# A rounding step by absolute value in bfloat16, and three of eight final tiles added by TensorE

## The chip, the core and the metric

The kernel runs on one NeuronCore of a Trainium2 chip. Five engines work side by side, each through its own queue in program order: TensorE (PE) multiplies matrices and writes to PSUM, VectorE (DVE) and ScalarE (ACT) work on tiles, GpSimd (POOL) here splits weights, and SyncE (SP) issues the transfers. They wait for one another by semaphores. The metric is the time of one execution on the device, in microseconds (us). Lower is better.

## The reference

`x` has 32 batches of 32 rows of 512. A per-batch 32x32 mix, chosen by a token, goes ahead of an attention block (32 heads, 8 key heads, rotary embedding, causal softmax, output projection), whose result is added to `x`. Then comes a second mix and one linear layer with values rounded to FP8, and that result is added as well:

```
x = x + attention(mix1(x))
y = mix2(x)
qinput, input_scale = per_tensor_quantize(y)       # scale = max|y| / 448
qinput = fp8_cast(qinput);  qw = fp8_cast(qweight)  # round to 3 mantissa bits
out = einsum(qinput * input_scale, qw * weight_scale) + bias
qout, out_scale = per_tensor_quantize(out)          # clip(out / scale, -448, 448)
x = x + qout * out_scale
```

Both quantizations need a maximum over the whole tensor, so each is a point that every tile has to reach before any can go on.

## The kernel before, in words

The 1024 rows are 8 tiles of 128 rows by 512 columns; `xacc` holds them in SBUF from the first load to the store. Up to about 496 us the attention runs, and TensorE is fed without a break. The order on each engine is written out by hand, function by function; waits are `wait_ge` on counting semaphores. The change touches the end of each engine's program.

Rounding to FP8 is done with additions. For a value v, ScalarE makes v and v times 2^20; from the latter `magic` keeps the exponent and sets one mantissa bit (an integer operation of VectorE), and two SCALAR_TENSOR_TENSOR of VectorE add and subtract the number, which leaves v rounded in bfloat16. `round_w8` (L1154) does it for four pieces of the weight matrix, between the last attention steps; ScalarE's part is `scale_w8` (L585). The loop at L1252 does it for the eight tiles of y: sum (L1257), difference (L1266), and, two tiles behind, the maximum of the layer's output (`f_largest`, L1240). `y_div` and `y_exp` are ScalarE's two outputs (L620, L624); tile 0's `y_exp` is made by VectorE (L1246).

TensorE's loop at L903: for tile 0 four products (L908) and the bias product (L910); for each later tile three products into the same bank whose values are overwritten and which keep the engine busy (`hold_clock`, L897), the bias product (L914), then four products (L917) once `y8_done` says that the tile is rounded. Then `spread_max(1)` (L891) transposes a column of maxima, so that each partition gets the maximum over all.

VectorE makes four columns from it, `col[:, 9:10]` the last of them. ScalarE's `f_divide` (L635) scales the eight tiles into `f_div`, VectorE clips each (`clip`, L1290), multiplies by the scale and adds `xacc` (`add_back`, L1295), and SP stores the tile (L348). The eight results lie in eight PSUM banks, `f_ps[0..7]` = banks 5, 0, 6, 7, 1, 2, 3, 4; before the spread writes to bank 5, ScalarE copies tile 0 to `f_keep`.

Of the kernel before, what the change touches and what calls it, by code (L numbers as in the profile page):

```python
# [78 lines left out]
def build(nc, x, itok, conds, wq, wk, wv, wo, qweight, w_scale, bias, consts, v_mem, out):  # L79
    with ExitStack() as ctx:  # L80
# [3 lines left out]
        def sem(name):  # L84
            return ctx.enter_context(nc.semaphore(name))
# [14 lines left out]
        with ExitStack() as products:  # L100
# [87 lines left out]
        scores_mm, s_turned, soft_step, exp_done = sem("scores_mm"), sem("s_turned"), sem("soft_step"), sem("exp_done")  # L188
        pv_mm, o_hi_done, o_lo_done, wo_mm, acc_done = (sem(n) for n in ("pv_mm", "o_hi_done", "o_lo_done", "wo_mm", "acc_done"))
        w8_scaled, w8_step, wT_mm, wT_done = sem("w8_scaled"), sem("w8_step"), sem("wT_mm"), sem("wT_done")  # L190
        y_mm, y_copied, y_amax, tail_mm, tail_vec = (sem(n) for n in ("y_mm", "y_copied", "y_amax", "tail_mm", "tail_vec"))
        y_div_done, y_exp_done, y8_magic, y8_sum, y8_done = (
            sem(n) for n in ("y_div_done", "y_exp_done", "y8_magic", "y8_sum", "y8_done"))
# [41 lines left out]
        y_exp = lambda t: wv_raw[1][:, t, :] if t < TPU else raw_o[:, t - TPU, :]  # L235
        f_div = y_exp
        f_keep = second_u[:]
        y_t = lambda t: y_kept[:, t, :] if t < TPU else y_ps[t][:]
        y_sum = [flat(p_tr), flat(s_nat[0])]
        tmp_scaled = [second_u[:], third_u[:]]  # L240
        tmp_sum = first_p[:]

        def left_part(h, i):

# [17 lines left out]
        def _(sp):  # L262
# [80 lines left out]
                sp.wait_ge(pv_mm, BPT * (2 * (KV - 2) + r + 1))  # L343
                load_values(KV - 1, r)

            for t in range(TILES):
                sp.wait_ge(result, t + 1)
                sp.dma_start(out_rows[t], xacc[:, t, :]).then_inc(dma_out, 16)  # L348
            sp.wait_ge(dma_out, 16 * TILES)

# [88 lines left out]
        def _(act):  # L439
# [145 lines left out]
            def scale_w8(c):  # L585
                act.wait_ge(dma_ffn, 16)
                if c >= 2:
                    act.wait_ge(w8_step, 3 * (c - 1))
# [39 lines left out]

            act.wait_ge(f_amax, 1)
            act.activation(f_keep, f_ps[0][:], ACT.Copy).then_inc(f_kept, 1)  # L630
            act.wait_ge(tail_vec, 9)

            def f_divide(t):

                act.activation(f_div(t), f_keep if t == 0 else f_ps[t][:], ACT.Copy,  # L635
                               scale=col[:, 9:10]).then_inc(f_div_done, 1)

            for t in range(TILES):
                f_divide(t)


        @block.tensor
        def _(pe):
# [199 lines left out]

            def turn_w8():

                pe.wait_ge(w8_step, 3 * KC)
# [38 lines left out]
            def spread_max(n):  # L885

                ps = w_ps[1] if n == 0 else f_ps[0]
                pe.wait_ge(tail_vec, 5 * n + 1)
                if n == 1:
                    pe.wait_ge(f_kept, 1)  # L890
# [12 lines left out]
            for t in range(TILES):  # L903
                if t == 0:
                    pe.wait_ge(wT_done, KC)
                    pe.wait_ge(y8_done, 1)
                    for c in range(KC):
                        pe.matmul(f_ps[t][:], y8[:, t, c * P:(c + 1) * P], wT[:, c, :], start=(c == 0), stop=False)  # L908
                    pe.wait_ge(bias_done, 2)
                    pe.matmul(f_ps[t][:], ones_r[:], bias_parts, start=False, stop=True).then_inc(f_mm, 1)  # L910
                else:

                    hold_clock(f_ps[t][:], 3)
                    pe.matmul(f_ps[t][:], ones_r[:], bias_parts, start=True, stop=False)  # L914
                    pe.wait_ge(y8_done, t + 1)
                    for c in range(KC):
                        mm = pe.matmul(f_ps[t][:], y8[:, t, c * P:(c + 1) * P], wT[:, c, :], start=False,  # L917
                                       stop=(c == KC - 1))
                    mm.then_inc(f_mm, 1)
            spread_max(1)  # L920


        @block.vector
        def _(dve):
# [229 lines left out]
            def round_w8(c):  # L1154

                dve.wait_ge(w8_scaled, c + 1)
                scaled, plain = tmp_scaled[c % 2], raw_w8[:, c, :]
                dve.tensor_scalar(scaled.bitcast(I32), scaled.bitcast(I32), EXP_BITS, HALF_BIT,
                                  ALU.bitwise_and, ALU.bitwise_or).then_inc(w8_step, 1)
                dve.wait_ge(w8_step, 3 * c + 1)  # L1160
                dve.scalar_tensor_tensor(out=tmp_sum, in0=scaled, scalar=LEAST, in1=plain, op0=ALU.max,
                                         op1=ALU.add).then_inc(w8_step, 1)
                dve.wait_ge(w8_step, 3 * c + 2)
# [64 lines left out]
            dve.wait_ge(tail_vec, 4)  # L1228
            dve.tensor_scalar(col[:, 2:3], col[:, 1:2], SHIFT, None, ALU.mult).then_inc(tail_vec, 1)

            def magic(t):

                if t > 0:
                    dve.wait_ge(y_exp_done, t)
                else:
                    dve.wait_ge(bias_step, 1)
# [12 lines left out]
            magic(0)  # L1249
            dve.wait_ge(bias_step, 2)  # L1250
            dve.reciprocal(col[0:BIAS_ROWS, 10:11], col[0:BIAS_ROWS, 8:9]).then_inc(bias_step, 1)
            for t in range(TILES):  # L1252


                dve.wait_ge(y_div_done, t + 1)
                dve.wait_ge(y8_magic, t + 1)
                dve.scalar_tensor_tensor(out=y_sum[t % 2], in0=y_exp(t), scalar=LEAST, in1=y_div(t), op0=ALU.max,  # L1257
                                         op1=ALU.add).then_inc(y8_sum, 1)
                if t == 0:
                    dve.wait_ge(bias_step, 3)  # L1260
                    dve.wait_ge(dma_ffn, 32)
                    dve.tensor_scalar(bias_sc, bias_row, col[0:BIAS_ROWS, 10:11], None, ALU.mult).then_inc(bias_done, 1)
                elif t < TILES - 1:
                    magic(t + 1)
                dve.wait_ge(y8_sum, t + 1)
                dve.scalar_tensor_tensor(out=y8[:, t, :], in0=y_exp(t), scalar=LEAST, in1=y_sum[t % 2], op0=ALU.max,  # L1266
                                         op1=ALU.subtract).then_inc(y8_done, 1)
                if t == 0:

                    dve.tensor_scalar(col[:, 5:6], col[:, 8:9], 1.0 / FP8_MAX, None, ALU.mult).then_inc(bias_step, 1)  # L1270
                    magic(1)
# [59 lines left out]
```

## Time and profile before

| | |
|---|---|
| time, median of 3 runs | 532.58 us (531.99 to 532.63) |
| the profiled execution | 532.47 us, span of its records 530.7 us |
| PE busy | 504.1 us (95%), 3150 products |
| DVE busy | 421.9 us (79%), 662 instructions |
| ACT busy | 247.9 us (47%), 475 instructions |
| POOL busy | 311.1 us (59%), 308 instructions |
| mean granted clock of TensorE | 0.988 |

The profile is of one execution. Its times count from the start of the span; 1.77 us of the execution lie outside it. A product of float32 leaves two records, others leave one. The record of a product contains its way through the array, so records overlap: what counts is the distance from start to start.

### The profile page before, as it was taken

How to read it: one execution, taken by the hardware profiler on the slowest of the kernel's cores; microseconds unless marked ns; L12 is line 12 of the kernel's file. 1: busy time of each engine (PE TensorE's matmuls, PEld its weight loads, DVE VectorE, ACT ScalarE, POOL GpSimd, SP SyncE). 2: the span in 40 equal slices, each digit the busy share in tenths (PEclk: the TensorE clock that was granted, in tenths of full speed). 3: DMA queues.
4: the chain of work that ended last, by engine and by line, in shares of the span. 5: the costliest groups of instructions: out<-in, count | busy, mean ns of one | idle time of the engine just before them, and what ended most of it. 6: DMA issues, size and time to landing. Idle time of an engine off the chain costs nothing.

```text
span 530.7 us, 9229 instructions
## 1 busy us (share of the span) xinstructions
PE 504.1 (95%) x3150; PEld 402.1 (76%) x3150; DVE 421.9 (79%) x662; ACT 247.9 (47%) x475; POOL 311.1 (59%) x308
## 2 busy tenths in 40 slices
PE   8988999998899999999999999999999999999990
PEld 6876877886688888888888888888888887788530
DVE  5469768796687969796979798978978788985796
ACT  2453454574163727472655346444635454333423
POOL 1238988689648765876597569756974653300000
PEclk9999999999899999999999999999999999999996
DMA  7315521220322031104020502040310005000004
GB/s 265 133 40 162 156 81 59 81 73 27 93 69 59 1 116 44 59 0 157 1 59 0 158 0 59 0 158 0 95 64 20 2 2 203 0 2 1 0 0 158
DMA packets 32644, 35.27 MB, mean 66 GB/s; under 512 B 2251, under 2 KB 22859, under 8 KB 32620
## 3 DMA queue, kind: packets, MB, share of 16 engines
q1 hardware_dynamic: 32620, 34.96, 20.5%
q8 instruction: 14, 0.23, 0.2%
q14 instruction: 10, 0.08, 0.0%
HBM read 28.66 MB, written 6.29 MB: 66 GB/s over the span
## 4 chain that ended last, share of the span: by engine, by line
PE 79%; POOL 11%; DVE 5%; issue 2%; ACT 1%; DMA 1%; DVEq 0%; ACTq 0%; POOLq 0%
PE bank L716 22%; PE bank L718 21%; PE bank L717 21%; POOL wq_lo L374 4%; PE bank L784 3%; PE bank L773 3%; POOL q_rot L388 2%; PE bank L840 1%; PE bank L659 1%; PE bank L917 1%; POOL o_lo L395 1%; POOL wo_lo L383 1%; PE bank L688 1%; DVE q_swap L1049 1%; PE bank L897 1%
## 5 line engine op out<-in xcount | busy, mean ns | idle before, releaser
L388 POOL TENSOR_TENSOR q_rot<-q_rot,q_swap 128x512 f32<-128x512 f32 x64 | 88.6, 1386 | 60.7 <-DVE q_swap L1049 60.7
L513 ACT ACTIVATE q_swap<-bank 64x512 f32<-64x512 f32 x80 | 47.6, 596 | 132.0 <-PE bank L718 84.5
L716 PE MATMUL bank<-wo_hi,o_hi 128*128 128x512 f32 x256 | 101.9, 398 | 4.4 <-issue 2.4
L718 PE MATMUL bank<-wo_hi,o_lo 128*128 128x512 f32 x256 | 100.5, 392 | 0.0
L717 PE MATMUL bank<-wo_lo,o_hi 128*128 128x512 f32 x256 | 100.3, 392 | 0.0
L1097 DVE TENSOR_TENSOR xacc<-xacc,bank 128x512 f32<-128x512 f32 x64 | 43.6, 682 | 37.5 <-PE bank L718 37.4
L1049 DVE TENSOR_TENSOR q_swap<-q_swap,cst 128x512 f32<-128x512 f32 x80 | 61.6, 769 | 0.0
L716 PEld LDWEIGHTS bank<-wo_hi,o_hi 128*128 128x128 f32 x256 | 48.3, 189 | 17.1 <-issue 4.8
L718 PEld LDWEIGHTS bank<-wo_hi,o_lo 128*128 128x128 f32 x256 | 48.3, 189 | 10.3
L717 PEld LDWEIGHTS bank<-wo_lo,o_hi 128*128 128x128 f32 x256 | 48.4, 189 | 9.6
L1048 DVE TENSOR_TENSOR q_rot<-bank,cst 128x512 f32<-128x512 f32 x64 | 43.8, 685 | 8.8 <-ACT q_swap L514 7.2
L383 POOL TENSOR_TENSOR wo_lo<-raw_o,wo_hi 128x512 fp32r<-128x512 f32 x32 | 45.0, 1429 | 9.7 <-ACT wo_hi L499 9.7
L716 PE MATMUL bank<-t_hi,wq_hi 128*128 128x512 f32 x128 | 49.8, 389 | 0.0
L718 PE MATMUL bank<-t_hi,wq_lo 128*128 128x512 f32 x128 | 49.8, 389 | 0.0
L717 PE MATMUL bank<-t_lo,wq_hi 128*128 128x512 f32 x128 | 49.8, 389 | 0.0
L374 POOL TENSOR_TENSOR wq_lo<-w_sum,wq_hi 128x256 fp32r<-128x256 f32 x64 | 48.4, 767 | 0.0
L514 ACT ACTIVATE q_swap<-bank 64x512 f32<-64x512 f32 x80 | 47.2, 591 | 0.9
L1090 DVE TENSOR_TENSOR o_lo<-bank,o_hi 128x512 fp32r<-128x512 f32 x64 | 39.6, 678 | 2.7 <-ACT o_hi L530 2.7
L374 POOL TENSOR_TENSOR wq_lo<-raw_q,wq_hi 128x256 fp32r<-128x256 f32 x48 | 36.7, 765 | 7.1 <-ACT wq_hi L482 7.1
L388 POOL TENSOR_TENSOR k_rot<-k_rot,q_swap 128x512 f32<-128x512 f32 x16 | 20.8, 1298 | 34.1 <-DVE q_swap L1049 34.1
L530 ACT ACTIVATE o_hi<-bank 128x512 fp32r<-128x512 f32 x64 | 33.1, 605 | 16.4 <-PE bank L784 16.1
L716 PE MATMUL bank<-hT_hi,wq_hi 128*128 128x512 f32 x96 | 39.1, 407 | 1.2 <-DVE v_st L963 1.0
(160 smaller groups left out, 1047.2 us busy)
## 6 DMA issues: line engine op xcount, KB each, us to landing
raw_q<-in_L_attn_wq SPq DMA_DIRECT2D x16, 512.0 KB, 3.9
raw_o<-in_L_attn_wo SPq DMA_DIRECT2D x8, 1024.0 KB, 7.4
v_st<-values SPq DMA_DIRECT2D x16, 256.0 KB, 4.4
xacc<-in_x SPq DMA_DIRECT2D x4, 512.0 KB, 7.0
raw_k<-in_L_attn_wk SPq DMA_DIRECT2D x8, 256.0 KB, 4.2
out<-xacc SPq DMA_DIRECT2D x8, 256.0 KB, 2.0
values<-v_more SPq DMA_DIRECT2D x6, 256.0 KB, 2.0
raw_o<-in_L_attn_wv SPq DMA_DIRECT2D x1, 1024.0 KB, 7.6
```

The source lines that it names most:

```text
L374: pool.tensor_tensor(wq_lo[:, i], left_part(h, i), wq_hi[:, i].bitcast(F32), ALU.subtract).then_inc(wq_lo_done, 1)
L383: pool.tensor_tensor(lo[:, h, :], raw_o[:, h, :], hi[:, h, :].bitcast(F32), ALU.subtract).then_inc(wo_lo_done, 1)
L388: pool.tensor_tensor(item_out(h, k), item_out(h, k), q_swap[(h + k) % 2][:], ALU.add).then_inc(rope_done, 1)
L513: act.activation(dst[0:P // 2, :], ps[P // 2:P, :], ACT.Copy)
L514: act.activation(dst[P // 2:P, :], ps[0:P // 2, :], ACT.Copy).then_inc(swap_done, 1)
L716: pe.matmul(dst, l_hi, r_hi, start=(i == 0), stop=False)
L717: pe.matmul(dst, l_hi, r_lo, start=False, stop=False)
L718: mm = pe.matmul(dst, l_lo, r_hi, start=False, stop=(i == n - 1))
L1048: dve.tensor_tensor(by_t(item_out(h, k)), by_t(item_ps[k][:]), cos_b, ALU.mult).then_inc(rope_cos, 1)
L1049: dve.tensor_tensor(by_t(q_swap[b][:]), by_t(q_swap[b][:]), sin_b, ALU.mult).then_inc(rope_mul, 1)
L1090: dve.tensor_tensor(by_batch(lo, b), by_tile(ps[b]), by_batch(hi, b).bitcast(F32), ALU.subtract).then_inc(o_lo_done, 1)
L1097: dve.tensor_tensor(xacc[:, tile, :], xacc[:, tile, :], w_ps[j % 2][:], ALU.add).then_inc(acc_done, 1)
```

## The change

In the rounding, ScalarE now writes `y_exp` and `tmp_scaled` as an absolute value in bfloat16 (Abs in place of Copy, a bfloat16 view on the same memory), and the integer operation is gone. Tile 0's `y_div` is made by VectorE and its `y_exp` by ScalarE, the other way round than before. `hold_clock` of a tile waits for `y_exp_done`.

In the last stretch the tiles 2, 4 and 6 (`BY_PE`) are added by TensorE: an identity product puts `xacc` into the banks of tiles 1, 2 and 3, whose values ScalarE has copied to SBUF before (`f_keep` for four tiles now); later a second product adds the clipped tile times an identity scaled by `col[:, 7:8]`, and ScalarE copies the bank to `xacc`. SP stores in the order `STORE_ORDER`.

```diff
-EXP_BITS = 0x7F800000
-HALF_BIT = 0x00400000
+BY_DVE, BY_PE = (0, 1, 3, 5, 7), (2, 4, 6)
+STORE_ORDER = (0, 1, 3, 2, 4, 5, 6, 7)
...
-        f_div = y_exp
-        f_keep = second_u[:]
+        f_div = lambda t: wv_raw[1][:, t, :] if t < TPU else raw_o[:, t - TPU, :]
+        y_exp = lambda t: f_div(t).bitcast(BF16)[:, 0:HID]
+        f_keep = lambda t: y_kept[:, t, :]
...
-        tmp_scaled = [second_u[:], third_u[:]]
+        tmp_scaled = [u[:].bitcast(BF16)[:, 0:HID] for u in (second_u, third_u)]
+        scaled_ident = first_p[:, 0:P]
...
-            for t in range(TILES):
-                sp.wait_ge(result, t + 1)
+            for t in STORE_ORDER:
+                if t in BY_PE:
+                    sp.wait_ge(act_result, BY_PE.index(t) + 1)
+                else:
+                    sp.wait_ge(result, BY_DVE.index(t) + 1)
...
-                act.activation(tmp_scaled[c % 2], raw_w8[:, c, :], ACT.Copy, scale=SHIFT).then_inc(w8_scaled, 1)
+                act.activation(tmp_scaled[c % 2], raw_w8[:, c, :], ACT.Abs, scale=SHIFT).then_inc(w8_scaled, 1)
...
                 if t == 0:
-                    act.wait_ge(tail_vec, 4)
-                act.activation(y_div(t), y_t(t), ACT.Copy, scale=col[:, 1:2]).then_inc(y_div_done, 1)
-                if t == 1:
                     act.wait_ge(tail_vec, 5)
-                if t > 0:
-                    act.activation(y_exp(t), y_t(t), ACT.Copy, scale=col[:, 2:3]).then_inc(y_exp_done, 1)
+                else:
+                    act.activation(y_div(t), y_t(t), ACT.Copy, scale=col[:, 1:2]).then_inc(y_div_done, 1)
+                act.activation(y_exp(t), y_t(t), ACT.Abs, scale=col[:, 2:3]).then_inc(y_exp_done, 1)
...
-            act.wait_ge(f_amax, 1)
-            act.activation(f_keep, f_ps[0][:], ACT.Copy).then_inc(f_kept, 1)
+            for t in range(TPU):
+                act.wait_ge(f_amax, t + 1)
+                act.activation(f_keep(t), f_ps[t][:], ACT.Copy).then_inc(f_kept, 1)
+
+            act.wait_ge(tail_vec, 8)
+            act.activation(scaled_ident, ident, ACT.Copy, scale=col[:, 7:8]).then_inc(spread, 1)
             act.wait_ge(tail_vec, 9)
...
+            for n, t in enumerate(BY_PE):
+                act.wait_ge(pe_sum, n + 1)
+                act.activation(xacc[:, t, :], f_ps[n + 1][:], ACT.Copy).then_inc(act_result, 1)
...
+                    pe.wait_ge(y_exp_done, t + 1)
                     hold_clock(f_ps[t][:], 3)
...
+            for n, t in enumerate(BY_PE):
+                pe.wait_ge(f_kept, n + 2)
+                pe.wait_ge(f_amax, n + 2)
+                pe.matmul(f_ps[n + 1][:], ident, xacc[:, t, :], start=True, stop=False)
             spread_max(1)
+            pe.wait_ge(spread, 1)
+            for n, t in enumerate(BY_PE):
+                pe.wait_ge(f_clip, t + 1)
+                pe.matmul(f_ps[n + 1][:], scaled_ident, f_div(t), start=False, stop=True).then_inc(pe_sum, 1)
...
-                dve.tensor_scalar(scaled.bitcast(I32), scaled.bitcast(I32), EXP_BITS, HALF_BIT,
-                                  ALU.bitwise_and, ALU.bitwise_or).then_inc(w8_step, 1)
...
-            def magic(t):
...
-                dve.tensor_scalar(y_exp(t).bitcast(I32), y_exp(t).bitcast(I32), EXP_BITS, HALF_BIT,
-                                  ALU.bitwise_and, ALU.bitwise_or).then_inc(y8_magic, 1)
...
-            dve.tensor_scalar(y_exp(0), y_t(0), col[:, 1:2], SHIFT, ALU.mult, ALU.mult).then_inc(bias_step, 1)
+            dve.tensor_scalar(y_div(0), y_t(0), col[:, 1:2], None, ALU.mult).then_inc(bias_step, 1)
...
-                magic(t + 1)
...
             clip(0)
-            for t in range(1, TILES):
-                clip(t)
-                add_back(t - 1)
-            add_back(TILES - 1)
+            clip(1)
+            add_back(0)
+            clip(2)
+            add_back(1)
+            clip(3)
+            add_back(3)
+            clip(4)
+            clip(5)
+            clip(6)
+            clip(7)
+            add_back(5)
+            add_back(7)
```

How the queues stand at the end of the program. First TensorE before, from tile 7's holding products on (`bank4` is tile 7's bank, `bank5` takes the spread; L897 is `hold_clock`, L914 the bias, L917 the tile's products, L891 the spread):

```order
L897 MATMUL bank4<-w8 128x512 x3
L914 MATMUL bank4<-wk_hi,ones_r 128x512
L917 MATMUL bank4<-wT,y8 128x512 [waits y8_done]
L917 MATMUL bank4<-wT,y8 128x512 x3
L891 MATMUL bank5<-cst,col 128x128 [waits f_kept,tail_vec]
```

And TensorE now, from the same place (L906, L924, L927 and L900 are the same four; `cst` is the identity, `first_p` the scaled identity):

```order
L906 MATMUL bank4<-w8 128x512 [waits y_exp_done]
L906 MATMUL bank4<-w8 128x512 x2
L924 MATMUL bank4<-wk_hi,ones_r 128x512
L927 MATMUL bank4<-wT,y8 128x512 [waits y8_done]
L927 MATMUL bank4<-wT,y8 128x512 x3
L933 MATMUL bank0<-xacc,cst 128x512 [waits f_amax,f_kept]
L933 MATMUL bank6<-xacc,cst 128x512 [waits f_amax,f_kept]
L933 MATMUL bank7<-xacc,cst 128x512 [waits f_amax,f_kept]
L900 MATMUL bank5<-cst,col 128x128 [waits tail_vec]
L938 MATMUL bank0<-raw_q,first_p 128x512 [waits f_clip,spread]
L938 MATMUL bank6<-raw_o,first_p 128x512 [waits f_clip]
L938 MATMUL bank7<-raw_o,first_p 128x512 [waits f_clip]
```

Three identity products stand between tile 7's products and the spread, and three more at the end, each behind a clip.

VectorE's last rows before (L1290 is `clip`, L1295 `add_back`), from tile 4's clip on:

```order
L1290 TENSOR_SCALAR raw_o<-raw_o 128x512 [waits f_div_done]
L1295 SCALAR_TENSOR_TENSOR xacc<-raw_q,col,xacc 128x512 [waits f_clip]
L1290 TENSOR_SCALAR raw_o<-raw_o 128x512 [waits f_div_done]
L1295 SCALAR_TENSOR_TENSOR xacc<-raw_o,col,xacc 128x512 [waits f_clip]
L1290 TENSOR_SCALAR raw_o<-raw_o 128x512 [waits f_div_done]
L1295 SCALAR_TENSOR_TENSOR xacc<-raw_o,col,xacc 128x512 [waits f_clip]
L1290 TENSOR_SCALAR raw_o<-raw_o 128x512 [waits f_div_done]
L1295 SCALAR_TENSOR_TENSOR xacc<-raw_o,col,xacc 128x512 [waits f_clip] x2
```

And now, from tile 2's clip on (L1299 and L1304):

```order
L1299 TENSOR_SCALAR raw_q<-raw_q 128x512 [waits f_div_done]
L1304 SCALAR_TENSOR_TENSOR xacc<-raw_q,col,xacc 128x512 [waits f_clip]
L1299 TENSOR_SCALAR raw_q<-raw_q 128x512 [waits f_div_done]
L1304 SCALAR_TENSOR_TENSOR xacc<-raw_q,col,xacc 128x512 [waits f_clip]
L1299 TENSOR_SCALAR raw_o<-raw_o 128x512 [waits f_div_done] x4
L1304 SCALAR_TENSOR_TENSOR xacc<-raw_o,col,xacc 128x512 [waits f_clip] x2
```

Clips 4 to 7 stand together, and only the adds of tiles 5 and 7 follow them.

## Rows read from the trace of the kernel before

**Rows 1.** Timeline, TensorE: start, length, line, tiles, shapes, count, idle before.
```profile
500.61 1.02 PE L908 MATMUL bank<-wT,y 128*128 128x512 bf16 x4 [0.46 <-DVE y L1266]
501.63 0.49 PE L910 MATMUL bank<-wk_hi,ones_r 33*128 33x512 f32 x1
...
503.30 1.04 PE L917 MATMUL bank<-wT,y 128*128 128x512 bf16 x4
504.17 0.81 PE L897 MATMUL bank<-w 128*128 128x512 bf16 x3
504.91 0.50 PE L914 MATMUL bank<-wk_hi,ones_r 33*128 33x512 f32 x1
...
515.56 1.04 PE L917 MATMUL bank<-wT,y 128*128 128x512 bf16 x4
517.58 0.49 PE L891 MATMUL bank<-cst,col 128*128 128x128 f32 x2 [0.98 <-DVE col L1217]
```

**Rows 2.** Timeline, VectorE, head of the rounding loop.
```profile
498.79 0.69 DVE L1257 SCALAR_TENSOR_TENSOR p_tr<-raw_q,y_divs 128x512 f32<-128x512 f32 x1
...
500.89 0.68 DVE L1274 TENSOR_TENSOR wk_hi<-k_rot,wk_hi 1x512 fp32r<-1x512 f32 x1
...
502.55 0.68 DVE L1266 SCALAR_TENSOR_TENSOR y<-raw_q,s_nat 128x512 bf16<-128x512 f32 x1
```

**Rows 3.** Timeline, ScalarE: the scaling, and two small ones earlier.
```profile
507.44 0.60 ACT L630 ACTIVATE second_u<-bank 128x512 f32<-128x512 f32 x1
519.13 0.72 ACT L635 ACTIVATE raw_q<-second_u,col 128x512 f32<-128x512 f32 x1 [11.09 <-DVE col L1286]
519.75 1.82 ACT L635 ACTIVATE raw_q<-bank,col 128x512 f32<-128x512 f32 x3
521.46 2.43 ACT L635 ACTIVATE raw_o<-bank,col 128x512 f32<-128x512 f32 x4
...
L472 ACT ACTIVATE ident_bf<-cst x1: 327/327/327, 35.9 to 35.9; 128x128 bf16<-128x128 f32 x1
```

**Rows 4.** Timeline, VectorE, last stretch: clip L1290, add L1295.
```profile
519.88 1.00 DVE L1290 TENSOR_SCALAR raw_q<-raw_q 128x512 f32<-128x512 f32 x2 [0.79 <-ACT raw_q L635]
520.80 0.75 DVE L1295 SCALAR_TENSOR_TENSOR xacc<-raw_q,col,xacc 128x512 f32<-128x512 f32 x1
521.46 0.42 DVE L1290 TENSOR_SCALAR raw_q<-raw_q 128x512 f32<-128x512 f32 x1
...
526.78 1.40 DVE L1295 SCALAR_TENSOR_TENSOR xacc<-raw_o,col,xacc 128x512 f32<-128x512 f32 x2
```

**Rows 5.** Stores by line; stretches: window, length, busy by engine, PEclk, DMA share, GB/s.
```profile
L348 SPq DMA_DIRECT2D out<-xacc x8: 332/332/362, 521.6 to 528.2; - x8
...
522.30:523.30 1.00, 0.00 (x0) 0.00 (x0) 1.00 (x3) 1.00 (x3) 0.00 (x0) 0.50 0.70 262
528.30:529.90 1.60, 0.00 (x0) 0.00 (x0) 0.00 (x0) 0.00 (x0) 0.00 (x0) 0.50 0.88 328
```

**Rows 6.** Timeline, ScalarE, head of the rounding loop.
```profile
497.67 1.34 ACT L620 ACTIVATE y_divs<-y_kept,col 128x512 f32<-128x512 f32 x2 [9.73 <-DVE col L1227]
...
499.90 0.63 ACT L627 ACTIVATE wk_hi<-k_rot 33x512 fp32r<-33x512 f32 x1 [0.28 <-DVE k_rot L1262]
```

**Rows 7.** Product records by line: ns min/median/max, first and last start, shapes.
```profile
L853 PE MATMUL bank<-ident_bf,w x16: 219/219/230, 485.2 to 486.1; 128*128 128x128 bf16 x16
...
L897 PE MATMUL bank<-w x39: 379/379/389, 495.3 to 514.8; 128*128 128x512 bf16 x39
...
L659 PE MATMUL bank<-wcond,selectors x64: 219/275/275, 5.9 to 14.7; 128*128 128x64 f32 x64
```

**Rows 8.** Stretches around the fall of the clock; columns as in rows 5.
```profile
517.00:521.00 4.00, 0.49 (x2) 0.30 (x2) 2.35 (x9) 1.87 (x4) 0.00 (x0) 1.00 0.00 0
...
521.20:530.70 9.50, 0.00 (x0) 0.00 (x0) 6.99 (x14) 2.69 (x5) 0.00 (x0) 0.50 0.59 221
```

**Rows 9.** Groups by line and form, TensorE: busy us, mean ns, idle before.
```profile
L647 PE MATMUL bank<-warm 128*128 128x512 bf16 x11 | 4.6, 604 | 1.5 <-DVE warm L925 1.5
```

More of the change, by code:

```diff
@@ L190, in build @@
         w8_scaled, w8_step, wT_mm, wT_done = sem("w8_scaled"), sem("w8_step"), sem("wT_mm"), sem("wT_done")
+        pe_sum, act_result, spread = sem("pe_sum"), sem("act_result"), sem("spread")
         y_mm, y_copied, y_amax, tail_mm, tail_vec = (sem(n) for n in ("y_mm", "y_copied", "y_amax", "tail_mm", "tail_vec"))
-        y_div_done, y_exp_done, y8_magic, y8_sum, y8_done = (
-            sem(n) for n in ("y_div_done", "y_exp_done", "y8_magic", "y8_sum", "y8_done"))
+        y_div_done, y_exp_done, y8_sum, y8_done = (
+            sem(n) for n in ("y_div_done", "y_exp_done", "y8_sum", "y8_done"))
         bias_step, bias_done, bias_hi_done = (sem(n) for n in ("bias_step", "bias_done", "bias_hi_done"))
@@ L234, in build @@
         y_div = lambda t: y_divs[:, t, :]
-        y_exp = lambda t: wv_raw[1][:, t, :] if t < TPU else raw_o[:, t - TPU, :]
-        f_div = y_exp
-        f_keep = second_u[:]
+        f_div = lambda t: wv_raw[1][:, t, :] if t < TPU else raw_o[:, t - TPU, :]
+        y_exp = lambda t: f_div(t).bitcast(BF16)[:, 0:HID]
+        f_keep = lambda t: y_kept[:, t, :]
         y_t = lambda t: y_kept[:, t, :] if t < TPU else y_ps[t][:]
         y_sum = [flat(p_tr), flat(s_nat[0])]
-        tmp_scaled = [second_u[:], third_u[:]]
+        tmp_scaled = [u[:].bitcast(BF16)[:, 0:HID] for u in (second_u, third_u)]
         tmp_sum = first_p[:]
+        scaled_ident = first_p[:, 0:P]
         def left_part(h, i):
@@ L587, in scale_w8 @@
                 if c >= 2:
-                    act.wait_ge(w8_step, 3 * (c - 1))
-                act.activation(tmp_scaled[c % 2], raw_w8[:, c, :], ACT.Copy, scale=SHIFT).then_inc(w8_scaled, 1)
+                    act.wait_ge(w8_step, 2 * (c - 1))
+                act.activation(tmp_scaled[c % 2], raw_w8[:, c, :], ACT.Abs, scale=SHIFT).then_inc(w8_scaled, 1)
             scale_w8(0)
@@ L627, in _ @@
                     act.activation(bias_parts, bias_sc, ACT.Copy).then_inc(bias_hi_done, 1)
-            act.wait_ge(f_amax, 1)
-            act.activation(f_keep, f_ps[0][:], ACT.Copy).then_inc(f_kept, 1)
+            for t in range(TPU):
[3 more added lines that the diff above has]
+            act.activation(scaled_ident, ident, ACT.Copy, scale=col[:, 7:8]).then_inc(spread, 1)
             act.wait_ge(tail_vec, 9)
             def f_divide(t):
-                act.activation(f_div(t), f_keep if t == 0 else f_ps[t][:], ACT.Copy,
+                act.activation(f_div(t), f_keep(t) if t < TPU else f_ps[t][:], ACT.Copy,
                                scale=col[:, 9:10]).then_inc(f_div_done, 1)
@@ L844, in turn_w8 @@
             def turn_w8():
-                pe.wait_ge(w8_step, 3 * KC)
+                pe.wait_ge(w8_step, 2 * KC)
                 pe.wait_ge(const_done, 1)
@@ L888, in spread_max @@
                 pe.wait_ge(tail_vec, 5 * n + 1)
-                if n == 1:
-                    pe.wait_ge(f_kept, 1)
                 pe.matmul(ps[:, 0:P], col[:, 4 * n:4 * n + 1].broadcast_to([P, P]), ident,
@@ L1157, in round_w8 @@
                 scaled, plain = tmp_scaled[c % 2], raw_w8[:, c, :]
-                dve.tensor_scalar(scaled.bitcast(I32), scaled.bitcast(I32), EXP_BITS, HALF_BIT,
-                                  ALU.bitwise_and, ALU.bitwise_or).then_inc(w8_step, 1)
-                dve.wait_ge(w8_step, 3 * c + 1)
+                if c > 0:
+                    dve.wait_ge(w8_step, 2 * c)
                 dve.scalar_tensor_tensor(out=tmp_sum, in0=scaled, scalar=LEAST, in1=plain, op0=ALU.max,
                                          op1=ALU.add).then_inc(w8_step, 1)
-                dve.wait_ge(w8_step, 3 * c + 2)
+                dve.wait_ge(w8_step, 2 * c + 1)
                 dve.scalar_tensor_tensor(out=w8[:, c, :], in0=scaled, scalar=LEAST, in1=tmp_sum, op0=ALU.max,
@@ L1229, in _ @@
             dve.tensor_scalar(col[:, 2:3], col[:, 1:2], SHIFT, None, ALU.mult).then_inc(tail_vec, 1)
-            def magic(t):
[L1233 to L1236, printed above, removed]
-                dve.tensor_scalar(y_exp(t).bitcast(I32), y_exp(t).bitcast(I32), EXP_BITS, HALF_BIT,
-                                  ALU.bitwise_and, ALU.bitwise_or).then_inc(y8_magic, 1)
             def f_largest(t):
@@ L1243, in f_largest @@
                                   apply_absolute_value=True).then_inc(f_amax, 1)
-            dve.tensor_scalar(y_exp(0), y_t(0), col[:, 1:2], SHIFT, ALU.mult, ALU.mult).then_inc(bias_step, 1)
+            dve.tensor_scalar(y_div(0), y_t(0), col[:, 1:2], None, ALU.mult).then_inc(bias_step, 1)
             dve.tensor_scalar(col[:, 8:9], col[:, 3:4], wsc[:, 0:1], None, ALU.mult).then_inc(bias_step, 1)
-            magic(0)
             dve.wait_ge(bias_step, 2)
@@ L1252, in _ @@
             for t in range(TILES):
-                dve.wait_ge(y_div_done, t + 1)
-                dve.wait_ge(y8_magic, t + 1)
+                if t == 0:
+                    dve.wait_ge(bias_step, 1)
+                else:
+                    dve.wait_ge(y_div_done, t)
+                if t >= 2:
+                    dve.wait_ge(y8_done, t - 1)
+                dve.wait_ge(y_exp_done, t + 1)
                 dve.scalar_tensor_tensor(out=y_sum[t % 2], in0=y_exp(t), scalar=LEAST, in1=y_div(t), op0=ALU.max,
@@ L1262, in _ @@
                     dve.tensor_scalar(bias_sc, bias_row, col[0:BIAS_ROWS, 10:11], None, ALU.mult).then_inc(bias_done, 1)
-                elif t < TILES - 1:
-                    magic(t + 1)
                 dve.wait_ge(y8_sum, t + 1)
@@ L1270, in _ @@
                     dve.tensor_scalar(col[:, 5:6], col[:, 8:9], 1.0 / FP8_MAX, None, ALU.mult).then_inc(bias_step, 1)
-                    magic(1)
                     dve.wait_ge(bias_hi_done, 1)
```

## The prediction

> **What bounds the kernel now.** I read the busy table first: TensorE works 95% of the span. The change touches only the last 76 us, so I then read the timeline of each engine there, and for every gap what ended it. Up to 496 us TensorE streams products without a gap worth naming; the four rounding passes over the weight matrix (`round_w8`, 458 to 483 us) run on VectorE beside them. What counts is the tail, in three stretches.
>
> In the rounding loop (500.6 to 516.4 us) TensorE has no gap. Tile 1's products start at 503.30, tile 7's at 515.56, so a tile takes 12.26 / 6 = 2.04 us: three clock-holding products (0.74, from 504.17 to 504.91), the bias product (0.43), four real products (0.87, from 503.30 to 504.17) [rows 1]. VectorE delivers tile 1 at 502.55 + 0.68 = 503.23, just in time [rows 2]; from there on the queue of TensorE sets the pace, not the rounding. Only the head of the loop hangs on VectorE: the bias product of tile 0 at 501.63 follows the end of L1274 at 500.89 + 0.68 = 501.57 [rows 1, 2].
>
> Next comes a chain of single steps: last maximum, its spread over partitions by TensorE at 517.58, then columns on VectorE until ScalarE can scale the first tile at 519.13 [rows 1, 3]. In the last stretch VectorE is the bound: clip and add-back of a tile take 1.00 us, 0.33 + 0.66 from start to start (520.80, 521.46, last pair to 526.78 + 1.40 = 528.18) [rows 4], and each store is issued as its tile ends. After the last add the two last stores run back to back until 529.9, and 0.87 us later the span ends [rows 5].
>
> **Part 1: the bit operation goes.** Twelve TENSOR_SCALAR of VectorE go (four over the weights, eight in the loop). Between start and start each costs what a clip costs, 0.33 us [rows 4], so 4 us of VectorE. Worth: the four over the weights nothing, TensorE streams beside them. The seven from tile 1 on nothing, since TensorE's 2.04 us per tile stand; VectorE would now need 0.60 to 0.71 for each of three operations and waits for products instead. The head gains. ScalarE's first Abs starts one column step later than its first Copy did (497.67 + 0.20), takes 0.71 [rows 6] and ends at 498.58; VectorE's first sum starts at 498.62 instead of 498.79 [rows 2]. The bias row follows at the same distance: ScalarE rounds it at 499.72 instead of 499.90 [rows 6], and L1274's successor, without two bit operations ahead, runs from 500.39 to 501.07. Tile 0's products start 0.17 earlier, at 500.44, last 0.87, and the bias product at 501.31 no longer waits. Then 0.43 + 0.74 + 0.43 to tile 1's products at 502.91 instead of 503.30. **Gain 0.39 us.** VectorE has tile 1 by about 502.4, so this holds. The added waits of TensorE on `y_exp_done` cost nothing: ScalarE makes a pair in about 1.24 us, TensorE asks for one every 2.04. If the bfloat16 output or input changed ScalarE's 0.71 or VectorE's 0.68, only this 0.39 moves; bounds 0 and 0.6.
>
> Could Abs need a new function table? The built program has one table load in all, as before; I give this no weight.
>
> **Part 2: three identity products ahead of the spread.** TensorE's queue now has, after tile 7, three f32 products of 128x512 (identity by `xacc`) and only then the spread of the maximum. Their own waits (`f_amax` and `f_kept` up to 4) are long fulfilled. Their price is nowhere in the trace, and it is a large term. An f32 product leaves two records. In bfloat16 a record takes 219 ns for 128 columns and 379 for 512: 0.417 ns per column over 166 [rows 7]. The first f32 record with 64 columns takes 219, so 53 / 64 = 0.83 ns per column [rows 7]. Two records of 512 columns: 2 x 0.427 = 0.85, I take 0.87 with the small gap seen in the other streams. The bound below is one cycle per column and record, 0.43 a product; above, the record's own 0.59 each, 1.19 a product. Tile 7's products end their turn at 515.56 - 0.39 + 0.87 = 516.04; three products make 518.65. Without them the spread would start at 517.58 - 0.39 = 517.19. **So it starts at 518.65, a loss of 1.07 us against before.** The chain behind it keeps its length: the first scaling starts at 519.13 + 1.07 = 520.20 [rows 3]. The scaled identity (128x128, 0.33 us [rows 3]) fits between the column that it waits for and the last column.
>
> The Trainium skill ("FP8 and Floating Point Precision", section TensorE Precision Notes) says that a true fp32 product makes four passes through the array. By that rule three products would cost 3 x 4 x 0.213 = 2.56 us (an estimate from that page's passes). The 64-column record above agrees with it.
>
> **Part 3: the last stretch.** VectorE drops three adds (3 x 0.66 = 1.98), and add 3 now directly follows its own clip and must wait for its end, 0.13 more. Positions: clip 0 at 519.88 + 1.07 = 520.95, clip 1 at 521.57 behind its scaling, add 0 521.90, clip 2 522.57, add 1 522.90, clip 3 523.57, add 3 524.03, clips 4 to 7 from 524.69 in steps of 0.33, adds 5 and 7 at 526.02 and 526.68 [rows 4]. VectorE ends at 527.43, 0.75 before the old end. But the end is no longer there. Tile 4's product waits for clip 4 (ends 525.11), tile 6's for clip 6 (525.78) and for tile 4's; ScalarE is done scaling at about 525.0 (eight in steps of 0.57 to 0.62 [rows 3]) and copies each result in 0.60 [rows 3]; `STORE_ORDER` puts store 7 behind store 6 on SP, 0.33 per issue [rows 5].
>
> **The clock decides what these products cost.** Before, the granted clock was 1.00 up to 521.0 and 0.50 from 521.2 on, about three us after TensorE's last record, with nothing behind it to suffer [rows 1, 8]. Now TensorE rests from about 519.1 to 523.05 (clip 2's end), longer than that, then does one product and rests again to 525.17. I take it that tiles 4 and 6 run at 1.2 GHz: 1.74 us each. For the price of that clock I have the warm-up products, 604 ns a record against 379 [rows 7, 9], and 427 against 213 for the streaming part.
> The Trainium skill ("TensorE: Matmul & The Clock Gate", Part 1: The HAM clock gate) says the clock is halved after idle and given back only after sustained work. The fall in the rows agrees; that a single product does not bring it back no run here shows. With the rule the time is the forecast's, without it the first rival's.
>
> Sum: product of tile 4 from 525.17 done at 525.17 + 0.18 + 1.74 = 527.09, copied and store 4 issued at 527.77. Tile 6 from 526.91 done at 528.83, copied by 529.47, store 6 at 529.51, store 7 at 529.84. A store's burst begins 0.83 after its issue and takes 0.70 of all DMA engines (share 0.70 of 1.00 us [rows 5]); store 6 ends at 531.04, store 7 behind it at 531.74, and 0.87 later the span is over: 532.6, against 530.7. That is +1.9. The profiled execution took 532.47 and the median is 532.58, 0.02% apart, so I keep to the profiled one: 532.47 + 1.9 = **534.4 us**.
>
> **Rivals.**
> 1. The clock holds at 2.4 GHz for tiles 4 and 6. Then store 4 is issued at 526.85, 5 at 527.18, 6 at 527.77, 7 at 528.10; four bursts of 0.70 queue from 527.68 to 530.48, span 531.35, +0.65: 533.1. If it falls between the two products: store 6 at 528.64, span 531.75, +1.05: 533.5. For it: the fall came 4.5 us after the dense work ended, with one short spread between, and the new gap after the dense work is 4.4 us. Against: the rest itself is longer, and the second rest adds to it.
> 2. The other side: an f32 product of 512 columns costs 0.43, not 0.87. Then the three identity products end at 517.33, the spread starts at 517.35, 0.23 earlier than before instead of 1.07 later, and everything in part 3 moves 1.30 forward, with shorter products besides: at half clock store 7's burst ends at about 529.2 (span 530.0, 531.8 us), at full clock 528.8 (531.4 us). It decides from about 0.5 us a product downwards. Against it: the 64-column record of 219.
> 3. The f32 products cost more than 0.87, because each loads its weights twice and the array switches type: up to 1.19 each. The spread comes 1 us later still: 535.3.
>
> **How the numbers follow.** Forecast 0.44, rival 1 0.32, rival 2 0.14, rival 3 0.10. A measurement of this kernel can tell about 0.2%, 1.07 us: faster is below 531.5, slower above 533.65. Faster: most of rival 2 at full clock, and a head gain larger than counted, 0.14. Same: rival 1 and the rest of rival 2, 0.37. Slower: forecast and rival 3, 0.49. The likeliest case alone spans 533.8 to 535.0. The range that leaves out 2 in 10 goes from 531.7 to 535.2.
>
> **What would show it.** In the changed kernel's profile: tile 1's products about 0.4 us earlier and again 2.04 us per tile; the spread's product about 2.6 us behind tile 7's last product, with VectorE waiting for it over 1.5 us; the granted clock at 0.50 when the products of tiles 4 and 6 run, their records near 1.0 us; VectorE done before ScalarE's last copy; stores 6 and 7 last and back to back. Wrong would be a spread at 517.2 to 517.4, or a clock of 1.00 in the last stretch, or a rounding loop whose period falls below 2.04.

## The result, and the profile after

The changed kernel is slightly slower, clear of the noise: its median is 534.55 us beside 532.53 us for the one before, a difference of 2.0. The ratio of the runs is 1.0041 with a 95% interval of 1.0028 to 1.0055; that is +2.2 us, between 1.5 and 2.9. The forecast was 534.4. The profiled execution spans 533.3 us against 530.7.

Two executions can't be laid on top of each other from their start, since the head of this kernel scatters: over all the profiles of this study the product of the first spread, which ends the common part, starts between 495.15 and 497.68 us (once at 501.60), in no relation to the edit. (In 11 of the 14 profiles the granted clock also falls to 0.50 for 3.4 us somewhere between 127 and 140 us, in the middle of the attention; the first spread of the three without it starts at 495.62, 495.82 and 501.60, so that is not what scatters the head.) Of the 2.6 us between the two profiles, 0.86 were lost there, ahead of everything that the change could move except the rounding of the weights. So I measure from the first spread to the end of the span, and call it the tail. For the kernel before, its row and the span:

```profile
core 0 of [0], span 530.7 us
...
496.43 0.49 PE L891 MATMUL bank<-cst,col 128*128 128x128 f32 x2 [0.33 <-DVE col L1217]
```

A tail of 530.7 - 496.43 = 34.27 us. The span is printed to 0.1 us, so a tail is known to about 0.05, and a difference of two tails to 0.1. TensorE's timeline in the changed kernel, same columns as [rows 1]:

```profile
core 0 of [0], span 533.3 us
...
497.29 0.49 PE L900 MATMUL bank<-cst,col 128*128 128x128 f32 x2 [0.33 <-DVE col L1234]
...
501.36 1.02 PE L917 MATMUL bank<-wT,y 128*128 128x512 bf16 x4 [0.35 <-DVE y L1276]
502.32 0.50 PE L919 MATMUL bank<-wk_hi,ones_r 33*128 33x512 f32 x1
...
503.93 1.04 PE L927 MATMUL bank<-wT,y 128*128 128x512 bf16 x4
...
516.21 1.04 PE L927 MATMUL bank<-wT,y 128*128 128x512 bf16 x4
517.08 2.74 PE L933 MATMUL bank<-xacc,cst 128*128 128x512 f32 x6
519.66 0.38 PE L900 MATMUL bank<-cst,col 128*128 128x128 f32 x2
524.04 2.05 PE L938 MATMUL bank<-raw_q,first_p 128*128 128x512 f32 x2 [4.00 <-DVE raw_q L1299]
526.07 3.37 PE L938 MATMUL bank<-raw_o,first_p 128*128 128x512 f32 x4
```

The tail is 533.3 - 497.29 = 36.01 us, 1.74 longer. Read it against [rows 1]: from the first spread to tile 1's products 6.64 us instead of 6.87; then (516.21 - 503.93) / 6 = 2.05 us per tile, unchanged; then the identity products from 517.08 to 519.66, and only then the spread. VectorE stands ready long before and waits (third row: 1.91 us for the product of L900):

```profile
517.28 0.69 DVE L1250 TENSOR_REDUCE f_max<-bank 128x1 f32<-128x512 f32 x1 [1.35 <-PE bank L927]
518.01 0.16 DVE L1234 TENSOR_REDUCE col<-f_max 128x1 f32<-128x8 f32 x1
520.08 0.29 DVE L1236 TENSOR_REDUCE col<-bank 128x1 f32<-128x128 f32 x1 [1.91 <-PE bank L900]
...
526.94 1.41 DVE L1304 SCALAR_TENSOR_TENSOR xacc<-raw_o,col,xacc 128x512 f32<-128x512 f32 x2
```

It ends at 528.35, 31.06 after the first spread; before it was 528.18 - 496.43 = 31.75 [rows 4]. VectorE did get shorter, and no longer ends the kernel. ScalarE's copies do, each waiting for a product:

```profile
526.12 0.60 ACT L650 ACTIVATE xacc<-bank 128x512 f32<-128x512 f32 x1 [0.17 <-PE bank L938]
528.18 0.60 ACT L650 ACTIVATE xacc<-bank 128x512 f32<-128x512 f32 x1 [1.46 <-PE bank L938]
529.48 0.60 ACT L650 ACTIVATE xacc<-bank 128x512 f32<-128x512 f32 x1 [0.70 <-PE bank L938]
```

The clock, in stretches of 0.20 us (columns as in [rows 5]), fell at about 522.1 and came back at about 528.9, during the third product. Tile 2's product ran at half clock too:

```profile
522.00:522.20 0.20, 0.00 (x0) 0.00 (x0) 0.20 (x1) 0.20 (x1) 0.00 (x0) 0.67 0.00 0
...
528.80:529.00 0.20, 0.20 (x2) 0.00 (x0) 0.00 (x0) 0.00 (x0) 0.00 (x0) 0.76 0.03 10
```

And the stores: the slowest lands after 3.0 us (2.1 before). The last four (tiles 4 to 7) are issued from 528.81 to 530.5, and the DMA engines move them without a gap from about 529.6 to 532.4, four times 0.70 us; the last store waits there for the three ahead of it:

```profile
L354 SPq DMA_DIRECT2D out<-xacc x8: 332/342/457, 523.6 to 530.5; - x8
...
DMA to landing us min/median/max: 2.0/2.4/3.0
...
530.00:531.00 1.00, 0.00 (x0) 0.00 (x0) 0.00 (x0) 0.07 (x1) 0.00 (x0) 1.00 1.01 379
```

### The profile page after: what moved, and what is told of

Its sections match the earlier page's. It is cut to its first block, busy times and chain, and to the rows that moved or that the text cites. A ratio compares the mean times of both kernels' runs of the same rounds, so it can differ in the third digit from the quotient of the medians.

```text
span 533.3 us, 9249 instructions
## 1 busy us (share of the span) xinstructions
PE 512.3 (96%) x3160; PEld 405.4 (76%) x3162; DVE 414.9 (78%) x647; ACT 251.8 (47%) x482; POOL 311.3 (58%) x308
## 4 chain that ended last, share of the span: by engine, by line
PE 80%; POOL 11%; DVE 3%; issue 2%; ACT 1%; DMA 1%; ACTq 0%; POOLq 0%; DVEq 0%
PE bank L727 21%; PE bank L729 20%; PE bank L728 20%; POOL wq_lo L380 4%; PE bank L795 3%; PE bank L784 3%; POOL q_rot L394 2%; PE bank L670 1%; PE bank L851 1%; PE bank L927 1%; POOL o_lo L401 1%; POOL wo_lo L389 1%; PE bank L938 1%; PE bank L699 1%; DVE q_swap L1067 1%
## 5 line engine op out<-in xcount | busy, mean ns | idle before, releaser
L1067 DVE TENSOR_TENSOR q_swap<-q_swap,cst 128x512 f32<-128x512 f32 x80 | 60.0, 750 | 0.0
L380 POOL TENSOR_TENSOR wq_lo<-w_sum,wq_hi 128x256 fp32r<-128x256 f32 x64 | 47.0, 744 | 0.0
```

Of the source, the lines that this page charges most:

```text
L380: pool.tensor_tensor(wq_lo[:, i], left_part(h, i), wq_hi[:, i].bitcast(F32), ALU.subtract).then_inc(wq_lo_done, 1)
L1067: dve.tensor_tensor(by_t(q_swap[b][:]), by_t(q_swap[b][:]), sin_b, ALU.mult).then_inc(rope_mul, 1)
```

## The experiments

A *hold* is one of the clock-holding products of `hold_clock`. All ratios are against executions of the kernel before on the same chip and beside the version's own, so ratios can be compared between rows better than medians can. Tails come from one profile each.

| version | median us | ratio (95%) | tail us |
|---|---|---|---|
| before | 531.7 to 532.5 | 1 | 34.27 |
| changed | 534.55 | 1.0041 (1.0028 to 1.0055) | 36.01 |
| rounding alone | 532.08 | 0.9991 (0.9957 to 1.0026) | 34.07 |
| TensorE adds alone | 535.01 | 1.0052 (1.0019 to 1.0085) | 36.35 |
| identity late | 532.48 | 0.9998 (0.9975 to 1.0021) | 33.78 |
| clock held | 533.59 | 1.0027 (0.9995 to 1.0060) | 35.08 |
| changed, two holds | 533.12 | 1.0018 (1.0003 to 1.0032) | 34.87 |
| before, two holds | 531.80 | 0.9994 (0.9982 to 1.0005) | 34.01 |
| identity late, two holds | 530.36 | 0.9963 (0.9950 to 0.9976) | 32.30 |
| identity late, one hold | 529.95 | 0.9951 (0.9936 to 0.9966) | 32.10 |
| the same again | 530.40 | 0.9961 (0.9948 to 0.9975) | 33.06 |
| identity late, no hold | 530.03 | 0.9955 (0.9939 to 0.9971) | 32.02 |
| two tiles by TensorE | 529.26 | 0.9950 (0.9935 to 0.9966) | 32.29 |
| two tiles, clock held | 529.51 | 0.9959 (0.9943 to 0.9975) | 31.97 |

**The two parts apart.** The first keeps the rounding change and undoes the last stretch:

```diff
-            for n, t in enumerate(BY_PE):
-                pe.wait_ge(f_kept, n + 2)
-                pe.wait_ge(f_amax, n + 2)
-                pe.matmul(f_ps[n + 1][:], ident, xacc[:, t, :], start=True, stop=False)
+            pe.wait_ge(f_kept, 1)
             spread_max(1)
```
(with the second products, ScalarE's copies and the two orders put back as before). The second is the kernel before with the last stretch of the changed one.

> The rounding change alone (Abs in bfloat16, no bit operation); the last stretch as in the kernel before. Theory (only the head of the rounding loop gains, the loop's pace is TensorE's): 0.4 us below the kernel before, about 532.1, tile period still 2.04 us. Rival A (VectorE's freed 4 us count): 1 us or more below, tile period under 2.0. Rival B (the rounding change itself costs, by bfloat16 operands or a later ScalarE): not below the kernel before.

> The bit operation kept, only the three tiles added by TensorE, identity products ahead of the spread. Theory (all the loss lies here): 2.3 us above the kernel before, about 534.8; the spread's product 2.6 us behind tile 7's last product; clock 0.50 at the last products. Rival (the loss needs both parts, by a meeting of the two): within 1 us of the kernel before.

The rounding alone: the tail is 0.20 shorter, half of the 0.4 expected, and the ratio can't tell it from nothing. Tile 1's products come 6.64 us behind the first spread, as in the changed kernel (6.87 before), and a tile takes 2.05 us. That VectorE's 4 us count (rival A) is out by this period. By the ratio rival B is not excluded, only by the tail.

```profile
core 0 of [0], span 530.7 us
...
496.63 0.49 PE L890 MATMUL bank<-cst,col 128*128 128x128 f32 x2 [0.33 <-DVE col L1217]
...
503.27 1.04 PE L917 MATMUL bank<-wT,y 128*128 128x512 bf16 x4
...
515.54 1.04 PE L917 MATMUL bank<-wT,y 128*128 128x512 bf16 x4
```

```profile
core 0 of [0], span 531.5 us
...
495.15 0.49 PE L903 MATMUL bank<-cst,col 128*128 128x128 f32 x2 [0.33 <-DVE col L1237]
...
515.16 2.74 PE L935 MATMUL bank<-xacc,cst 128*128 128x512 f32 x6
517.73 0.38 PE L903 MATMUL bank<-cst,col 128*128 128x128 f32 x2
```

The adds alone (these rows) carry the whole loss: tail +2.08 (2.3 expected), median 535.01, the spread 2.57 us behind the start of the identity products, and a clock of 0.50 from 520.8 to 527.5. The tails of the two parts, -0.20 and +2.08, add up to 1.88 beside the 1.74 of both.

**The identity products behind the spread.**

```diff
+            pe.wait_ge(f_kept, TPU)
+            spread_max(1)
             for n, t in enumerate(BY_PE):
                 pe.wait_ge(f_kept, n + 2)
                 pe.wait_ge(f_amax, n + 2)
                 pe.matmul(f_ps[n + 1][:], ident, xacc[:, t, :], start=True, stop=False)
-            spread_max(1)
```

> The changed kernel with the three identity products moved behind the spread's product. Theory: the spread starts 0.4 us earlier than before instead of 0.8 later, and the identity products fill TensorE's rest, so the clock stays at 1.00 for the last products: 2.7 us below the changed kernel, 0.8 below the one before, about 531.7. Rival (the identity products' place costs nothing, since the end waits for stores or VectorE): like the changed kernel, 534.5. If only the place counts and the clock falls all the same: 533.0.

```profile
core 0 of [0], span 529.4 us
...
495.62 0.49 PE L900 MATMUL bank<-cst,col 128*128 128x128 f32 x2 [0.33 <-DVE col L1235]
...
516.63 0.46 PE L900 MATMUL bank<-cst,col 128*128 128x128 f32 x2 [1.07 <-DVE col L1235]
516.93 2.74 PE L935 MATMUL bank<-xacc,cst 128*128 128x512 f32 x6
521.09 1.10 PE L939 MATMUL bank<-raw_q,first_p 128*128 128x512 f32 x2 [1.42 <-DVE raw_q L1300]
523.12 1.98 PE L939 MATMUL bank<-raw_o,first_p 128*128 128x512 f32 x4 [0.93 <-DVE raw_o L1300]
```

The second spread now starts 21.01 us after the first instead of 22.37 (changed) and 21.15 (before). The clock stayed at 1.00 until 528.7, behind TensorE's last product, and the record of a product that stands alone is 1.10 us long instead of 2.05. The tail is 2.23 shorter than the changed kernel's. The theory is borne out in kind; in size it is 0.5 short of its 2.7. The ratio shows no gain against the kernel before, but its interval (about -1.3 to +1.1 us) has room for the 0.5 of the tails. The clock may also have fallen in part of the executions, as it did in a profile further below; that was not shown here.

**The clock held, nothing moved.**

```diff
+            pe.wait_ge(tail_vec, 7)
+            hold_clock(f_ps[0][:], 15)
             pe.wait_ge(spread, 1)
```

> The changed kernel with 15 products more, whose result is overwritten, between the spread and the last products (bank of tile 0), so that TensorE has no long rest. Theory (the half clock of the last products costs 1.2 us): about 533.3, last products' records near 0.6 us, spread as late as in the changed kernel. Rival (clips, copies or stores set the end, the clock does not count): 534.5.

```profile
core 0 of [0], span 530.9 us
...
495.82 0.49 PE L900 MATMUL bank<-cst,col 128*128 128x128 f32 x2 [0.33 <-DVE col L1236]
...
518.18 0.38 PE L900 MATMUL bank<-cst,col 128*128 128x128 f32 x2
518.95 3.41 PE L906 MATMUL bank<-w 128*128 128x512 bf16 x14 [0.39 <-DVE col L1238]
522.56 1.10 PE L940 MATMUL bank<-raw_q,first_p 128*128 128x512 f32 x2 [0.20 <-DVE raw_q L1301]
524.59 1.98 PE L940 MATMUL bank<-raw_o,first_p 128*128 128x512 f32 x4 [0.93 <-DVE raw_o L1301]
```

The spread is as late as in the changed kernel (22.36), the products are short, the tail is 0.93 shorter than the changed kernel's (expected 1.2). So about 0.9 of the loss is the clock. The later spread costs 1.2 more, and about 0.4 comes back, presumably from VectorE's dropped adds and the shorter head: 0.93 + 1.22 - 0.41 = 1.74. Clock and place together, 0.93 + 1.36 (22.37 - 21.01) = 2.29, make about the 2.23 of the version above.

**Who sets the pace of the rounding loop.** One number changed, in the changed kernel and in the one before:

```diff
-                    hold_clock(f_ps[t][:], 3)
+                    hold_clock(f_ps[t][:], 2)
```

> The changed kernel with two clock-holding products per tile instead of three. Theory (the loop's pace is TensorE's queue, 2.04 us a tile, while VectorE now needs only 1.92): TensorE's tile takes 1.83 us, tile 7's products start 1.3 us earlier, 1.3 us below the changed kernel, about 533.2 beside 534.5. Rival (VectorE or ScalarE sets the pace, or the clock falls with fewer products): no gain, 534.5 or more.

> The kernel before with two clock-holding products per tile. Theory (with the bit operation VectorE needs 2.14 us a tile, so it takes over as the bound): tile 7's products start only 0.3 us earlier, 532.0 beside 532.3, TensorE waits for the rounding at each tile. Rival (the bit operation is not what counts, the third holding product is the whole cost): 1.3 us below.

In the changed kernel a tile takes (513.86 - 502.86) / 6 = 1.83 us and the tail is 1.14 shorter, with the clock at 0.50 for its last products, as in the changed kernel:

```profile
502.86 1.04 PE L927 MATMUL bank<-wT,y 128*128 128x512 bf16 x4
...
513.86 1.04 PE L927 MATMUL bank<-wT,y 128*128 128x512 bf16 x4
```

In the kernel before the same edit brings 0.26 in the tail and nothing that the ratio can tell; TensorE waits for the rounding (idle before, last column), 2.14 us from tile to tile:

```profile
509.27 1.04 PE L917 MATMUL bank<-wT,y 128*128 128x512 bf16 x3 [0.23 <-DVE y L1266]
...
511.41 1.04 PE L917 MATMUL bank<-wT,y 128*128 128x512 bf16 x4 [0.24 <-DVE y L1266]
```

The difference, 1.14 beside 0.26, is what the missing bit operation is worth, and it is had only where TensorE's queue is shortened with it. Both expectations held to 0.2 us.

**Both mended, then fewer holds.** The identity products stand behind the spread as in the edit above, and the loop has two, one or no holding product per tile.

> Identity products behind the spread and two clock-holding products per tile. Theory: the gains of the two edits add up, 0.5 and 1.3 us below the kernel before, about 530.5 beside 532.3; clock 1.00 to the end of TensorE's work. Rival (the last stores run back to back, so a faster loop is given back there): 1 us or less below the kernel before.

> As the version with identity products behind the spread, but one clock-holding product per tile. Theory: VectorE's 1.92 us a tile is the bound now, tile 7's products start 0.2 us earlier than with two, about 530.3, and TensorE waits for the rounding at each tile. Rival (the clock falls, since TensorE works a smaller share): tile products at half speed, above the kernel before.

> As the version with identity products behind the spread, but no clock-holding product in the loop. Theory (VectorE's 1.92 us a tile is the bound): same time as with one, 530.0. Rival (TensorE, busy two thirds of the loop, loses its clock): granted clock 0.50 somewhere between 500 and 520 us, 532 or more.

> The version with identity products behind the spread and one clock-holding product per tile once more, beside the two others of this call; its first profiled execution had lost 5 us ahead of the loop, as single executions do. Both theories: ratio near 0.995; the stretch from the first spread to the end 32.1 us again, the head without the loss.

Both mends together are 2.0 to 2.6 us below the kernel before, clear of the noise: all four intervals end below 0.998. Between two, one and no hold nothing can be told. With none the clock stayed at 1.00 in the loop, and from tile 3 on a tile takes 1.93 us, VectorE's time; TensorE is busy for 11.40 of the 14.24 us from 501.76 to 516. The repeat of the version with one hold gave the same ratio but not the same tail: 33.06 instead of 32.10, for the same program. Its rows show the cause:

```profile
core 0 of [0], span 529.1 us
...
496.04 0.49 PE L900 MATMUL bank<-cst,col 128*128 128x128 f32 x2 [0.33 <-DVE col L1235]
...
515.62 2.74 PE L935 MATMUL bank<-xacc,cst 128*128 128x512 f32 x6
519.79 1.10 PE L939 MATMUL bank<-raw_q,first_p 128*128 128x512 f32 x2 [1.42 <-DVE raw_q L1300]
521.82 3.44 PE L939 MATMUL bank<-raw_o,first_p 128*128 128x512 f32 x4 [0.94 <-DVE raw_o L1300]
...
521.20:521.40 0.20, 0.00 (x0) 0.00 (x0) 0.20 (x2) 0.20 (x1) 0.00 (x0) 0.93 0.89 338
521.40:521.60 0.20, 0.00 (x0) 0.00 (x0) 0.20 (x2) 0.20 (x2) 0.00 (x0) 0.50 1.11 420
```

Here the clock fell at 521.4 and came back at 524.8, and the last two products took 3.44 us instead of 1.98. TensorE had rested 1.42 us and then, behind tile 2's product, half a microsecond before it fell. Work behind the spread does not secure the clock; whether it falls differs between executions of one program.

**Fewer tiles for TensorE.** Tile 6 goes back to VectorE, on top of the version with one hold:

```diff
-BY_DVE, BY_PE = (0, 1, 3, 5, 7), (2, 4, 6)
-STORE_ORDER = (0, 1, 3, 2, 4, 5, 6, 7)
+BY_DVE, BY_PE = (0, 1, 3, 5, 6, 7), (2, 4)
+STORE_ORDER = (0, 1, 3, 2, 5, 4, 6, 7)
...
             clip(5)
+            add_back(5)
             clip(6)
             clip(7)
-            add_back(5)
+            add_back(6)
```

> Identity products behind the spread, one clock-holding product per tile, and only tiles 2 and 4 added by TensorE (6 goes back to VectorE); stores in the order 0, 1, 3, 2, 5, 4, 6, 7. Theory (with three such tiles the last four stores are issued within 1.3 us and their bursts of 0.70 us queue): VectorE ends 0.7 us later, but the last burst ends 0.8 us earlier than in the version with three; 529.2 beside 530.0. Rival (VectorE's chain sets the end again): 0.3 us or more above the version with three.

```profile
core 0 of [0], span 527.5 us
...
495.21 0.49 PE L900 MATMUL bank<-cst,col 128*128 128x128 f32 x2 [0.33 <-DVE col L1235]
...
520.98 2.07 PE L939 MATMUL bank<-raw_o,first_p 128*128 128x512 f32 x2 [0.77 <-DVE raw_o L1300]
```

The clock had fallen here too (the product took 2.07), so its like is the repeat: 32.29 against 33.06, the 0.8 expected. The DMA engines are full at the end for about 2.1 us, three stores, where the repeat has about 2.9 us, four stores; this fits the theory. Against 32.10, where the clock stayed at 1.00, it is no gain, and the ratios of the three overlap. Its median, 529.26, is the lowest of all, 0.50% below the kernel before, but with these intervals that is no ranking. The last run adds products that hold the clock:

```diff
+            pe.wait_ge(tail_vec, 7)
+            hold_clock(f_ps[0][:], 8)
             pe.wait_ge(spread, 1)
             for n, t in enumerate(BY_PE):
+                if n == 1:
+                    hold_clock(f_ps[0][:], 4)
                 pe.wait_ge(f_clip, t + 1)
```

> The version with two tiles by TensorE, with 8 overwritten products between its identity products and tile 2's, and 4 between tile 2's and tile 4's, so that TensorE rests less than 1 us at a time. Theory (in that version's profile the clock had fallen to 0.50 ahead of tile 4's product, which took 2.07 us instead of 1.1, and store 4 came late into the queue): clock 1.00 for both, store 4's burst about 0.9 us earlier, the end 0.3 to 0.4 earlier, about 0.995 of the kernel before or below. Rival (VectorE's last add and store 7 set the end): no change against 32.29 us from the first spread to the end.

The clock was 1.00, tile 4's product took 1.1 us and the tail 31.97, 0.32 less, as expected; the ratio shows nothing of it. Here the stores have become the limit: from 523.6 to 527.2 the DMA engines move one store behind the other, with a busy share of 1.02 from 524 to 526 us.

## Why the prediction was right

**The head.** Forecast -0.39, measured -0.23 (6.64 instead of 6.87 us), in the right place and mis-sized. The bias product of tile 0 no longer waited for L1274's successor, but it came 0.96 us behind the first product of its tile (501.36, 502.32), not the 0.87 that I took from the running stream; tile 0 follows a pause, which may be why. And VectorE's first sum started 0.06 later than assumed behind ScalarE's first Abs.

**The loop.** 2.05 us per tile (2.04 before), with VectorE idle 1.35 us before its last maximum. The two-hold pair shows that it is TensorE's queue.

**Identity products.** Forecast 2.61 us for three, measured 517.08 to 519.66 = 2.58. The second spread lies 22.37 us behind the first, before 21.15: +1.22, forecast +1.07; the difference is the head's. The second rival (0.43 a product) and the third (1.19) are out. The estimate from the four passes that the Trainium skill names ("FP8 and Floating Point Precision", section TensorE Precision Notes) was 2.56; the trace agrees. The first scaling came 0.11 sooner behind the spread than before; the spread's product, which now followed others without a pause, has a record of 0.38 us instead of 0.49.

**The clock.** It fell, as forecast, and tiles 2 and 4 and part of tile 6 ran at half of it. Two sizes were off, in opposite directions. Tile 4's product started right behind its clip, as forecast, and ended 2.07 us later (526.07 to 528.14, where ScalarE's copy follows 0.04 behind); the forecast was 1.74 and 0.18 for its way out, 1.92. The 1.74 itself was right for records in a row. At half clock they start 0.85 us apart, at full clock 0.43 (2.58 / 6); what was missing is the longer first record of a product that had to wait, 1.02 us to the next (526.07, 527.09). From the run with two holds, whose last product lies wholly at half clock, two views that start with its first and its second record:

```profile
525.59 1.91 PE L938 MATMUL bank<-raw_o,first_p 128*128 128x512 f32 x2
...
526.44 1.06 PE L938 MATMUL bank<-raw_o,first_p 128*128 128x512 f32 x1
```

And the clock came back at 528.9, so tile 6's product ended 1.30 us behind tile 4's instead of the 1.74 taken. The last copy started 32.19 us after the first spread, forecast 528.87 - 496.43 = 32.44. I had taken it that nothing brings the clock back in this stretch; that was wrong. The Trainium skill ("TensorE: Matmul & The Clock Gate", Part 1: The HAM clock gate) has it return after sustained work, and the trace agrees: these were products with almost no gap.

**The end.** From the last store's issue to the end 2.8 us, as the queueing bursts gave it (531.74 + 0.87 - 529.84 = 2.77). Tail in sum: forecast +1.9, measured +1.74. By the ratio the time rose 2.2 us, with 1.9 inside its interval. The mechanism was right but for the clock's return. That the sum came within 0.2 us is in part luck, since sizes missed either way: the second spread came 0.15 later than forecast, the scaling behind it 0.11 sooner, tile 4's product took 0.15 more and the distance to tile 6's end was 0.44 less.

**What stays open.** The changed kernel's 13 executions scatter more (532.9 to 539.0) than the 13 before (531.3 to 533.3), but in the larger set beside the first four versions the kernel before scattered as widely (531.1 to 538.8 in 35). The fall of the clock hardly explains it. The mean granted clock of each execution is 0.989 to 0.995 for all 13 of the changed kernel, while the six profiles in which the clock held through the last products have 0.996 to 0.999. So it probably fell in all of them, and executions with nearly the same mean, 0.989 and 0.990, took from 532.9 to 539.0 us. What scatters is not known. The fear that the bfloat16 operands change ScalarE's or VectorE's durations did not come true: 0.71 and 0.69 as in [rows 2, 6].

## What to carry to other kernels

Work that is handed to an idle engine has to stand in its queue behind everything that others wait for: the same three products made the spread 1.2 us late when they stood ahead of it, and not at all when they stood behind it. An engine that is busy with filler looks like the bound and hides what a cut elsewhere is worth; look for overwritten results first, and shorten both sides together. Give an engine that rests for microseconds no work at the end of the critical chain, unless the sum still holds at its half clock.

## What the runs showed of the hardware that was not expected

- A float32 product of 128x512 takes 0.86 us in a row at full clock, two records 0.43 apart; at half clock the records are 0.85 apart, twice that. One that stands alone takes 1.10 us to its end at full clock and 2.05 at half.
- Three such products with almost no gap, 524.04 to 529.44, brought the granted clock back to 1.00 at 528.9, 4.9 us after they began. In the repeat of the version with one hold it came back at 524.8, 3.0 us after two products without a gap had begun at 521.82. In the version with two tiles by TensorE, with one product from 520.98 to 523.05 and nothing behind, it did not come back before the end of the span.
- One program was seen with the clock at 1.00 through its last products in one execution and at 0.50 from 521.4 in another, although TensorE had rested at most 1.42 us at a time there.
- A loop without filler, in which TensorE works 11.4 of 14.2 us and rests up to 0.47 us at a time, kept the clock at 1.00.
